# Both halves' down products of an expert block in one PSUM bank, and one addition for both

## What is computed

```python
xn = layernorm(x)
attn = softmax(mask(q @ k.T * 8 ** -0.5)) @ v @ w_proj + b_proj
gates = scatter(softmax(top2(xn @ Wg.T)))
h = gelu(xn @ W1[e] + b1[e])          # 128 -> 512
o = h @ W2[e] + b2[e]                 # 512 -> 128, the "down" product
out = x + attn + sum_e gates[e] * o[e]
```

## Time and profile before

| | |
|---|---|
| profiled execution | 850.34 us |
| its span, first to last instruction | 848.6 us |
| around the span | 1.74 us |
| median of three runs | 850.88 us |
| instructions | 15145 |
| mean granted TensorE clock | 0.904 of 2.4 GHz |

### The profile page before, as it was taken

The page is one execution under the profiler, slowest core; times in us unless marked ns, Lnnn a source line. Parts: engine busy times, 40 slices in busy tenths (PEclk is TensorE's granted clock), DMA queues, the critical chain, the costliest instruction groups (busy, mean ns, idle before and its releaser), DMA issues.

```text
span 848.6 us, 15145 instructions
## 1 busy us (share of the span) xinstructions
PE 724.0 (85%) x5018; PEld 413.0 (49%) x5018; DVE 550.9 (65%) x2138; ACT 450.2 (53%) x715; POOL 301.7 (36%) x477
## 2 busy tenths in 40 slices
PE   0889889887887798788989899788999898998985
PEld 0745445443443545455555455445555456565433
DVE  5666676765555476667676666667666667667656
ACT  0224734414334467566576657566666657566543
POOL 6532620466775033342324122332314122323401
PEclk9966975968887699999999889999989999899988
DMA  9452850211315807044443507044433517030262
GB/s 234 98 121 86 184 142 4 54 44 44 91 48 145 259 22 214 13 116 121 108 117 93 146 22 210 13 114 124 128 97 92 147 37 219 16 104 17 77 167 74
DMA packets 95652, 88.34 MB, mean 104 GB/s; under 512 B 8528, under 2 KB 83064, under 8 KB 95576
## 3 DMA queue, kind: packets, MB, share of 16 engines
q1 hardware_dynamic: 90680, 77.27, 33.9%
q0 software_dynamic: 4544, 9.35, 3.4%
q10 hardware_dynamic: 352, 0.78, 0.4%
HBM read 50.18 MB, written 21.32 MB: 84 GB/s over the span
## 4 chain that ended last, share of the span: by engine, by line
PE 66%; DVE 21%; issue 5%; ACT 4%; DMA 1%; another core or an unknown queue 1%; POOL 0%; ACTq 0%; SPq 0%; DVEq 0%; POOLq 0%
PE aux L836 16%; PE ov L868 16%; PE aux L926 10%; PE aux L878 7%; DVE maxes L1060 5%; DVE maxes L1064 4%; PE sc L790 3%; PE sc L791 2%; PE sc L792 2%; DVE junk L1065 2%; ACT probs L743 2%; DVE xrow L1116 2%; PE sc L854 2%; PE aux L883 1%; PE aux L906 1%
## 5 line engine op out<-in xcount | busy, mean ns | idle before, releaser
L743 ACT ACTIVATE probs<-sc 128x1024 f32<-128x1024 f32 (+3 forms) x384 | 296.3, 811 | 232.1 <-PE sc L854 208.3
L836 PE MATMUL aux<-kT,qT 32*128 32x512 f32 (+3 forms) x768 | 226.4, 462 | 70.5 <-DVE maxes L1060 17.5
L652 POOL TENSOR_SCALAR_AFFINE_SELECT probs<-probs 128x256 f32<-128x256 f32 x256 | 104.6, 415 | 383.0 <-ACT probs L743 379.3
L1060 DVE TENSOR_REDUCE maxes<-aux 128x1 f32<-128x512 f32 x256 | 163.4, 684 | 57.0 <-PE aux L836 51.4
L836 PEld LDWEIGHTS aux<-kT,qT 32*128 32x128 f32 x768 | 102.6, 195 | 189.9 <-DVE maxes L1060 41.8
L1064 DVE TENSOR_REDUCE maxes<-aux 128x1 f32<-128x128 f32 (+2 forms) x384 | 161.2, 420 | 46.1 <-PE aux L836 40.9
L868 PE MATMUL ov<-probs,v 128*32 128x512 f32 (+3 forms) x1536 | 181.2, 546 | 0.7 <-POOL probs L652 0.2
L854 PE MATMUL sc<-qT,kT 32*128 32x512 f32 (+3 forms) x768 | 163.0, 446 | 7.5 <-DMA qT<-mT 3.0
L1065 DVE CUSTOM_DVE_ANT_0 junk<-aux,cst 128x128 f32<-128x128 f32 x512 | 139.1, 282 | 18.5 <-PE aux L836 18.4
L677 POOL DMA_INDIRECT ys<-ysb,back x78 | 75.9, 973 | 82.3 <-DVE ysb L1103 39.4
L878 PE MATMUL aux<-wh 128*128 128x384 f32 x339 | 92.4, 401 | 9.5 <-DVE maxes L1060 6.9
(11 more groups left out here) (119 smaller groups left out, 626.7 us busy)
## 6 DMA issues: line engine op xcount, KB each, us to landing
w1b<-w_scr SPq DMA_DIRECT2D x39, 512.0 KB, 4.4
w2all<-in_L_ffn_W SPq DMA_DIRECT2D x39, 256.0 KB
xs<-ysb SPq DMA_DIRECT2D x13, 387.0 KB, 7.0
xrow<-in_L_attn_x SPq DMA_DIRECT2D x8, 512.0 KB, 6.6
kT<-kqh SPq DMA_DIRECT2D x32, 128.0 KB, 2.8
w_scr<-w1b SPq DMA_DIRECT2D x8, 512.0 KB, 5.0
qT<-kqh SPq DMA_DIRECT2D x30, 128.0 KB, 2.7
xsin<-xs SPq DMA_DIRECT2D x6, 516.0 KB
```

The source lines that it names most:

```text
L652: nc.gpsimd.affine_select(out=block_, in_=block_, compare_op=ALU.is_ge, fill=0.0, base=0, pattern=[[0, 2], [1, P]], channel_multiplier=-1) ...
L743: nc.scalar.activation(probs[:, s % 2, 2 * half:2 * half + 2, 0:cols], pair(part)[:, :, 0:cols], ACT.Exp).then_inc(sc_done, 1)
L836: nc.tensor.matmul(bank(part)[:, 0:cols], qT[n % 3][rows, P * i:P * i + P], kT[n % 3][rows, k0:k0 + cols], start=True, stop=True).then_inc ...
L1060: nc.vector.reduce_max(maxes[:, i, slot, h:h + 1], bank(part)[:, 0:cols], axis=AX.X).then_inc(aux_d, 1)
```

## The change

The schedule hangs a whole block (both halves) on one step: steps 2, 4, 7 for three blocks, steps 2, 4, 6, 8 for four. One part "down" now has 8 matmuls into columns 0 to 127 and 128 to 255 of one bank, and one increment of aux_ready behind the last. VectorE makes one addition of 128x256 instead of two of 128x128. GpSimd still makes two sends per block, both one step behind the down part. array_use counts 4096 columns for the part, and fill distributes its warm matmuls by that.

```diff
-    subs = [(b, u) for b in blocks_of(f) for u in range(BK // P)] if f is not None else []
-    step_of = (2, 3, 4, 5, 7, 8) if len(subs) == 6 else range(2, 2 + len(subs))
+    subs = [(b,) for b in blocks_of(f)] if f is not None else []
+    step_of = (2, 4, 7) if len(subs) == 3 else (2, 4, 6, 8)
...
         if subs and s - 1 in step_of:
-            parts.append(("send", f) + subs[step_of.index(s - 1)])
+            parts.extend(("send", f) + subs[step_of.index(s - 1)] + (u,) for u in range(BK // P))
...
-    "project": 2048, "down": 2048, "rows": 256,
+    "project": 2048, "down": 4096, "rows": 256,
...
-                    pool.wait_ge(aux_d, D_AFTER["down", f, b, u])
+                    pool.wait_ge(aux_d, D_AFTER["down", f, b])
...
-                    for ch in range(CH):
-                        last_ = nc.tensor.matmul(bank(part)[:, 0:C], hid[:, i, ch, P * u:P * u + P],
-                                                 w2b[i][:, ch, :], start=(ch == 0), stop=(ch == CH - 1))
+                    for u in range(BK // P):
+                        for ch in range(CH):
+                            last_ = nc.tensor.matmul(bank(part)[:, C * u:C * u + C], hid[:, i, ch, P * u:P * u + P],
+                                                     w2b[i][:, ch, :], start=(ch == 0), stop=(ch == CH - 1))
                     last_.then_inc(aux_ready, 1)
...
-                    if i == 0 and u == 0:
+                    if i == 0:
                         for lane in range(SPARE):
                             wait(dve, returned[lane], 16 * sent(lane, f))
-                    nc.vector.tensor_tensor(ysb[:, BK // P * i + u, :], bank(part)[:, 0:C], bias[i][:, CH:CH + C],
-                                            ALU.add).then_inc(aux_d, 1)
+                    us = BK // P
+                    nc.vector.tensor_tensor(ysb[:, us * i:us * i + us, :],
+                                            bank(part)[:, 0:C * us].rearrange("p (u c) -> p u c", c=C),
+                                            mid(bias[i][:, CH:CH + C], us), ALU.add).then_inc(aux_d, 1)
```

More of the change, by code:

```diff
@@ L273, in array_use @@
         return MAXES[part[2] // HG][2] // 4
-    return {"turn": 1024, "xt": 1024, "columns": 1024, "rows_in": 1024, "project": 2048, "down": 2048, "rows": 256,
+    return {"turn": 1024, "xt": 1024, "columns": 1024, "rows_in": 1024, "project": 2048, "down": 4096, "rows": 256,
             "qk": 3 * W, "vg": 9 * (C + E), "hidden": 12 * BK}.get(what, 0)
@@ L567, in _ @@
                         if user_before(f, i):
-                            sp.wait_ge(aux_d, D_AFTER[("down",) + user_before(f, i) + (1,)])
+                            sp.wait_ge(aux_d, D_AFTER[("down",) + user_before(f, i)])
                         sp.dma_start(w2b[i], W2[bass.ds(experts[b], 1)].rearrange("o (c p) h -> p (o c) h", p=P)) \
@@ L750, in _ @@
                     if user_before(f, i):
-                        act.wait_ge(aux_ready, AUXI[("down",) + user_before(f, i) + (1,)] + 1)
+                        act.wait_ge(aux_ready, AUXI[("down",) + user_before(f, i)] + 1)
                     else:
@@ L920, in _ @@
                 elif what == "down":
-                    f, b, u = part[1:]
+                    f, b = part[1:]
                     pe.wait_ge(sc_done, PAIRI["hidden", f, b] + 1)
```

## The result

| | before | after |
|---|---|---|
| median | 849.56 us (4 runs) | 874.83 us (4 runs) |
| range | 847.46 to 859.74 | 871.44 to 883.24 |
| profiled execution, its span | 850.34, 848.6 us | 873.59, 871.8 us |
| mean granted clock in it | 0.904 | 0.889 |

The ratio is 1.0288, with a 95% interval of 1.0176 to 1.0399. The same two kernels on another chip gave 1.0335 (1.0259 to 1.0412): the change makes the kernel about 3% slower. (The ratios leave disturbed runs out.) 865.6 us was forecast, 852 to 883 as the range.

A forecast was written before the change was run, and what follows sets the result against it. The prediction took TensorE's instruction stream, with short hand-shakes to VectorE, as the bound. 848.6 + 6.3 (first three terms and warm matmuls) + 8.5 + 0.5 (sends) = 863.9 us span, 865.6 with 1.74 around it; range 852 to 883.

The forecast's parts named there:

- the warm matmuls: On TensorE's stream, 49 more warm matmuls at 0.19 us each: +9.3 us, the least being 0.
- the first three terms: Moved down products -2 us, longer addition +1.4 us, hand-shakes behind removed additions -2.4 us.
- The sends: Paired sends in POOL's queue stall PE 1.7 us in five three-block units, +8.5 us; four-block units +0.5 us.
- Rival B: Sends in POOL's queue hold nothing up, so the time is 856.6 us; chance 0.2.
- The moved down products: On PE, 39 downs move from light steps to steps that have one, -0.05 us each: -2 us.
- The longer addition: On DVE, 0.424 us replaces 0.292; uncovered only at 11 downs of step 4: +1.4 us.
- the hand-shakes: PE's 0.25 us waits for removed additions: no gain counted; 22 places behind warm matmuls at 0.11 us: -2.4 us.
- Rival C: At third max products behind 39 removed additions, waits of 0.25 us vanish, -9.8 us, giving 840.5 us; chance 0.1.
- the last sentence of the prediction: A different number of low-clock stretches at unit heads would move time about 4 us each, without any step being wrong.
- Rival A: Step 10's stall lowers the clock, 4 us each in three of five three-block units: 877.6 us; chance 0.2.
- the forecast's upper end: Part of the forecast's own 861 to 870 us lying above 868, where slower begins; stall 1.2 to 2.6 us.

The follow-up runs named there:

- e1: The changed kernel with the send of a block's second half one step later than the first's; ratio to the kernel before 1.0067.
- e5: The changed kernel with the third block of three at step 6 instead of 7, sends still paired; ratio to the kernel before 1.009.
- e6: The changed kernel with its two sends split and the warm matmuls placed as in the kernel before; ratio to the kernel before 0.9963.
- e3: The kernel before with the changed kernel's places of downs, sends and warm matmuls, each half keeping its own bank and addition; ratio to the kernel before 1.0318.
- e10: e6 with five more warm matmuls at the heads of units 4 to 14, run beside e9 on one chip; ratio to the kernel before 0.9896.
- e9: The kernel before with five more warm matmuls at the heads of units 4 to 14; ratio to the kernel before 0.9895.
- e4: The changed kernel run again without edits, for a second trace; ratio to the kernel before 1.0335.
- e2: The changed kernel with the warm matmuls placed as in the kernel before; ratio to the kernel before 1.0186.

## Why the prediction was right, and where it was not

865.6 us was forecast and 873.59 measured in the profiled execution, inside the range. The steps as forecast add 6.3 + 8.5 + 0.5 = 15.3 us, and at the full clock the steps of the stretch grew by 14. That the sum is so near is partly luck: the warm matmuls were priced too high, and the first three terms gained less than was counted. The clock, some 13 us, stood in no term.

**The sends: right in kind and size.** The stall of PE was worked out as 1.7 us from the earlier trace rows; the timeline has 1.63. The picture drawn from POOL's rows came out to the tenth: sends 1.28 us apart, selects right behind. Three small things were off. The down of step 8 was taken at 1.09 us, where the earlier trace rows have 0.92 for this one; step 8 became 0.94 us shorter. Splitting the sends gains 1.3 us a unit, not 1.7, since one send ahead of the selects keeps 0.35 us of the wait. And in units with four blocks the pair costs 1.9 us in all, not 0.5, behind step 10 rather than in it. Together 8.4 us by steps, for which 9.0 were forecast. Rival B (no stall) is ruled out by e1 and e5.

**The warm matmuls: mis-sized.** The term "+9.3 us" took 0.19 us for each of 49. The traces give 0.11 where there are six more in a unit, and 5.5 to 7 us for all, for they stand partly in the wait for the longer addition. That wait was the second term of the same sum: I counted it as covered by the warm matmuls and the matmuls at full price, which counts the cover twice.

**The moved down products: the price was off, and it didn't show.** The second half of a heavy step was put between 0.92 and 1.09 us, and all moves together at 2 us gained. Ahead of a warm matmul a whole block takes 619.17 - 617.47 = 1.70 us where a half took 0.92, so the second half takes only 0.78. Yet e6, which has these places and the old fill, takes 492 us at the full clock, and the kernel before 493: what PE saves in these rows it waits elsewhere.

**The longer addition and the hand-shakes.** The addition took 0.425 us for 0.424. 39 additions less give PE nothing, as the sum had assumed for the 0.25 us waits: max products wait for the addition in fewer places, and for earlier max parts in more. The 2.4 us that the sum did count behind warm matmuls don't show either. In the stretch, before and then after:

```profile
PEld aux L836 <- DVE maxes L1065: 24.5, 43, 1.0
...
PEld aux L836 <- DVE maxes L1060: 15.7, 31, 1.1
PEld aux L836 <- DVE ysb L1103: 15.4, 61, 0.4
```

```profile
PEld aux L836 <- DVE maxes L1066: 34.7, 64, 1.1
...
PEld aux L836 <- DVE maxes L1061: 21.6, 38, 1.1
...
PEld aux L836 <- DVE ysb L1105: 6.0, 19, 0.4
```

The waits for max parts rose from 40.2 to 56.3 us, those for the addition fell from 15.4 to 6.0; part of the rise is the lower clock. e6's steps are within 0.2 us of the kernel before's over eight steps, and e3 shows the merging at nothing. Rival C, in which the hand-shakes were the price, falls by e3 and by e10 against e9.

**The clock: the step that failed.** The forecast's sum had no term for it, and the last sentence of the prediction put a different number of low stretches at the heads outside all steps. In fact it is about half: some 13 of the 27.5 us in the stretch, by 0.94 against 0.97. Its price was off too. Rival A and that last sentence have 4 us for each low stretch; eleven and twelve of them cost 25 us, so 2 us each on average. Rival A had the kind and nearly the sum (877.6 us; 873.59 profiled, 874.83 median), but not the place, and its nearness is luck: of eleven and twelve low stretches two each follow the stall in step 10, and those cost 1 to 2.4 us each there, while nine stand at heads of units, where four or five stood before. The steps alone, 14 us, would have been 1.7%. So slower by over 2%, to which 0.40 was given, came about by the clock and not by the forecast's upper end.

**What is open.** That paired sends lower the clock is shown twice, by the mean clock of all runs of a kernel: 0.881 (e4) against 0.897 (e1), and 0.888 (e2) against 0.900 (e6). These are from two chips, on which the kernel before had 0.894 and 0.893. That the added warm matmuls do too is weaker: 0.888 against 0.881 with the pairs, 0.900 against 0.897 without. How a wait in step 10 comes to lower the clock at the head of the next unit, some 15 us later, no run settles. The head of unit 4, ahead of which no block has been worked on and no pair stands, was low in both traces after and in one of two before, so part of the count is chance. In the units with four blocks the longer last interval stands right before a head, but I haven't tried it alone.

## What to carry to other kernels

When two small pieces of work are joined, look first at what moves with them: here the gain was sought in a bank and an addition, and the loss came from a pair of sends in another engine's queue, ahead of an instruction with a deadline, and from matmuls that the fill put in by its own count. In GpSimd's queue, where the selects shown start only behind the sends ahead of them, what counted was not the length of what was put together but what stood next behind it; the same pair a step away from the next needed select cost nothing in the units with three blocks (e5). And where the granted clock is below full in a stretch, compare time and clock before pricing instructions: five matmuls a unit that fill a wait gave 1% (e9), where the merged bank gave nothing.

## What the runs showed of the hardware beyond that

A stretch at the lower clock costs less than half of its length in this kernel. By the sums of steps 31 and 34 us of low clock cost 11 and 13 us, 68 us cost 25 and 26 in the traces after, and 34 us cost 13 in e1: 0.37 to 0.4 us for each. PE also waits for other engines in these stretches, and such time need not grow with a lower clock, but no run here separates that. So the product of time and granted clock understates what was added by steps, 10 us by the product and 14 by the steps. And the spread of the runs themselves, 848 to 875 us for one unchanged kernel on one chip, goes with the mean clock: 0.909 at 848.12 us, 0.875 at 875.04.
